# Expansion one-hots made by ScalarE, the aggregate's compares read from PSUM, and the softmax in one PSUM bank, in a five-stage graph kernel

## What is computed

```python
m = xl[src] + xr[dst] + edge_attr @ We.T
score = jnp.where(m > 0, m, 0.2 * m) @ att
smax = jax.ops.segment_max(score, dst, num_segments=N)
es = jnp.exp(score - smax[dst])
denom = jax.ops.segment_sum(es, dst, num_segments=N)
alpha = es / (denom[dst] + 1e-16)
out = jax.ops.segment_sum(alpha[:, None] * xl[src], dst, num_segments=N)
```

## Time and profile before

| | |
|---|---|
| median of 3 runs | 13644.97 us (13634.25 to 13649.05) |
| the profiled execution's own time | 13576.47 us |
| its span, first to last instruction | 13574.4 us |
| PE, PEld | 77%, 64% of the span busy |
| POOL, DVE, ACT | 68%, 63%, 18% |
| mean granted TensorE clock, of full speed | 0.573 |
| HBM traffic | 65 GB/s over the span |

### The profile page before, as it was taken

One profiled execution on the slowest core, in us unless ns is written; L12 is line 12 of the kernel. 1 busy time (PEld: TensorE's weight loads), 2 busy tenths in 40 slices (PEclk: granted clock), 3 DMA queues, 4 the chain that ended last, 5 costly groups with the idle time before them and its releaser, 6 DMA issues. The chain is left out here.

```text
span 13574.4 us, 346433 instructions
## 1 busy us (share of the span) xinstructions
PE 10504.2 (77%) x102671; PEld 8732.6 (64%) x102672; DVE 8519.3 (63%) x15786; ACT 2406.7 (18%) x4954; POOL 9220.1 (68%) x8386
## 2 busy tenths in 40 slices
PE   2388888857888888488888857888888578888872
PEld 1377777746777777377777735777777357777762
DVE  7567777755777777355555544777777446666664
ACT  0011212111111122022222211111111112222220
POOL 0177777756777776577777735777777257777761
PEclk9855556555555555555555555555555555555555
DMA  0333333323333332222222223232222233333320
GB/s 16 84 75 71 73 73 73 73 42 75 72 72 73 73 71 57 39 55 54 55 54 55 54 54 106 77 78 77 77 78 72 69 96 78 78 78 78 78 64 11
DMA packets 771899, 912.63 MB, mean 67 GB/s; under 512 B 400125, under 2 KB 447616, under 8 KB 769760
## 3 DMA queue, kind: packets, MB, share of 16 engines
q0 software_dynamic: 267232, 390.16, 15.0%
q1 hardware_dynamic: 503008, 498.92, 13.0%
HBM read 791.99 MB, written 96.35 MB: 65 GB/s over the span
## 5 line engine op out<-in xcount | busy, mean ns | idle before, releaser
L914 POOL DMA_INDIRECT bs_gat<-table_b,bs_idx x1568 | 1750.7, 1117 | 506.5 <-issue 477.5
L914 POOL DMA_INDIRECT ds_gat<-table_d,ds_idx x1568 | 1749.3, 1116 | 506.7 <-issue 506.7
L914 POOL DMA_INDIRECT as_gat<-table_a,as_idx x1568 | 1740.9, 1110 | 506.6 <-issue 477.5
L914 POOL DMA_INDIRECT es_gat<-table_e,es_idx x1568 | 1725.7, 1101 | 505.6 <-issue 505.6
L914 POOL DMA_INDIRECT cs_gat<-table_c,cs_idx x1568 | 1731.0, 1104 | 491.0 <-issue 491.0
L1174 PE MATMUL ds_psM<-dstW_d,ds_hot 128*128 x9408 | 1252.7, 232 | 194.4 <-DVEq L1107 72.2
L1174 PE MATMUL es_psM<-dstW_e,es_hot 128*128 x9408 | 1253.5, 226 | 175.9 <-issue 65.3
L1174 PE MATMUL cs_psM<-dstW_c,cs_hot 128*128 x9408 | 1232.0, 183 | 182.3 <-DVEq L1100 68.9
L1174 PEld LDWEIGHTS ds_psM<-dstW_d,ds_hot 128*128 128x128 bf16 x9408 | 972.2, 103 | 481.6 <-issue 241.1
L1174 PEld LDWEIGHTS es_psM<-dstW_e,es_hot 128*128 128x128 bf16 x9408 | 962.6, 102 | 480.8 <-issue 224.4
L1174 PEld LDWEIGHTS cs_psM<-dstW_c,cs_hot 128*128 128x128 bf16 x9408 | 967.5, 103 | 473.0 <-issue 223.3
(11 more groups left out here) (758 smaller groups left out, 17937.2 us busy)
## 6 DMA issues: line engine op xcount, KB each, us to landing
as_rank<-rel_d SPq DMA_DIRECT2D x196, 256.0 KB
as_ea<-in_eaT SPq DMA_DIRECT2D x196, 256.0 KB
bs_rank<-rel_d SPq DMA_DIRECT2D x196, 256.0 KB
bs_ea<-in_eaT SPq DMA_DIRECT2D x196, 256.0 KB
cs_rank<-rel_d SPq DMA_DIRECT2D x196, 256.0 KB, 3.2
ds_rank<-rel_d SPq DMA_DIRECT2D x196, 256.0 KB, 3.3
es_rank<-rel_d SPq DMA_DIRECT2D x196, 256.0 KB, 3.4
table_e<-et_st SPq DMA_DIRECT2D x49, 544.0 KB, 2.7
```

The costliest lines, as they stand in the source:

```text
L914: g_.indirect_dma_start(gat[s][:, j, :], None, table, bass.IndirectOffsetOnAxis(ap=idxS[s][:, j:j + 1].bitcast(U32), axis=0)).then_inc(got ...
```

## The change

- `rel` is kept as fp32 instead of bf16, and the interleaved table `rankX` is replaced by `iota`, the numbers 0 to 255, which DVE copies once a stream into a PSUM bank of its own, `psI`.
- `collect_hot` becomes eight compares, one a tile: `psI` (fp32, 256 columns) against one column of `rel`. `ahot` is stored tile by tile, so that the weights of a collect matmul are contiguous; they had a step of 8 elements.
- The expansion's one-hots move from DVE to ACT, as max(0, 1 - (rank - p)²) by two Square and two Relu instructions of 1024 columns, with the partition's number as a pointer bias. They stand at the end of ACT's step.
- The softmax's transposes all go to `psX`, since `psY` gives up its bank to `psI`. The transposing of the next scores waits for `alphad` (alpha copied out) where it waited for `lowered`, and the wait for `alphad` before `give_ends` is left out.

```diff
-            rel=sb("rel", [P, TILES], BF16),
+            rel=sb("rel", [P, TILES]),
-            rankX=sb("rankX", [P, 2 * P, GROUP], BF16),
-            pid=sb("pid", [P, 2]),
+            iota=sb("iota", [P, 2 * P]),
+            pidN=sb("pidN", [P, 2]), one=sb("one", [P, 1]),
...
-        ahot = [sb(f"ahot{s}", [P, 2 * P, GROUP], BF16) for s in range(2)]
+        off = sb("off", [P, 2, GE], BF16)
+        ahot = [sb(f"ahot{s}", [P, GROUP, 2 * P], BF16) for s in range(2)]
...
-        psX, psY = ps("psX"), ps("psY")
+        psX, psI = ps("psX"), ps("psI")
...
             @block.scalar
+                def onehot(it, s):
+                    g = it * RING + s
+                    a.wait_ge(fed[s % 4], it * (3 * FEED) + (s // 4) * FEED + FEED)
+                    wait(a, made, g - 1)
+                    wait(a, hots, g)
+                    for x in range(2):
+                        a.activation(off[:, x, :], rank[s % 4][:, :], ACT.Square, bias=m["pidN"][:, x:x + 1]).then_inc(apart, 1)
+                    for x in range(2):
+                        a.wait_ge(apart, g * 2 + (x + 1))
+                        last = a.activation(hot[s % 2][:, x, :], off[:, x, :], ACT.Relu, bias=m["one"][:, 0:1], scale=-1.0)
+                    last.then_inc(hots, 1)
...
                     if i == 3 and r == 3 and within(xc, CHUNKS):
                         a.wait_ge(backed, xc + 1)
-                        a.activation(alpha[xs][:, 0, :], psY[:, 384:384 + CT], ACT.Copy).then_inc(alphad, 1)
+                        a.activation(alpha[xs][:, 0, :], psX[:, 256:256 + CT], ACT.Copy).then_inc(alphad, 1)
+                    if within(u + 2, GROUPS):
+                        if known(u):
+                            onehot((u + 2) // RING, (u + 2) % RING)
+                        else:
+                            onehot(it if s + 2 < RING else it + 1, (s + 2) % RING)
+                onehot(0, 0)
+                onehot(0, 1)
...
             @block.vector
+                v.tensor_copy(psI[:, 0:2 * P], m["iota"][:, :]).then_inc(xch, 1)
...
-                    for a in range(2):
-                        last = v.tensor_scalar(hot[s % 2][:, a, :], rank[s % 4][:, :], m["pid"][:, a:a + 1], None, ALU.is_equal)
-                    last.then_inc(hots, 1)
...
                 def collect_hot(k, ks):
                     wait(v, summed, k * 2 - 2)
-                    v.tensor_tensor(ahot[ks % 2][:, :, :], over(m["rel"][:, bass.ds(k * GROUP, GROUP)], 1, [P, 2 * P, GROUP]),
-                                    m["rankX"][:, :, :], ALU.is_equal).then_inc(ahots, 1)
+                    for j in range(GROUP):
+                        last = v.tensor_scalar(ahot[ks % 2][:, j, :], psI[:, 0:2 * P], m["rel"][:, bass.ds(k * GROUP + j, 1)], None, ALU.is_equal)
+                    last.then_inc(ahots, 1)
...
             @block.tensor
-                                    last = pe.matmul(sums[h][a][:, bass.ds(w, 1), :], ahot[ks % 2][:, a * P:(a + 1) * P, j],
+                                    last = pe.matmul(sums[h][a][:, bass.ds(w, 1), :], ahot[ks % 2][:, j, a * P:(a + 1) * P],
...
                     if r == 1 and live:
-                        wait(pe, alphad, xc)
                         give_ends(ended, xc + 1, gaveE)
...
                     if r == 0 and live:
                         pe.wait_ge(scored, xc * CG + CG)
-                        wait(pe, lowered, xc)
+                        wait(pe, alphad, xc)
```

More of the change, by code:

```diff
@@ L322, in _ @@
                                 base=0, pattern=[[1, P]], channel_multiplier=-1).then_inc(made, 1)
-                g.iota(m["rankX"][:, :, :], pattern=[[1, 2 * P], [0, GROUP]], base=0, channel_multiplier=0,
+                g.iota(m["iota"][:, :], pattern=[[1, 2 * P]], base=0, channel_multiplier=0,
                        allow_small_or_imprecise_dtypes=True).then_inc(made, 1)
@@ L328, in _ @@
                        allow_small_or_imprecise_dtypes=True).then_inc(made, 1)
-                g.iota(m["pid"][:, :], pattern=[[P, 2]], base=0, channel_multiplier=1,
+                g.memset(m["one"][:, :], 1.0).then_inc(made, 1)
+                g.iota(m["pidN"][:, :], pattern=[[-P, 2]], base=0, channel_multiplier=-1,
                        allow_small_or_imprecise_dtypes=True).then_inc(made, 1)
@@ L848, in stream @@
         masked = [sem(f"masked{s}") for s in range(3)]
-        hots, made, took, scored, sch, xch, ready, blank, wl, pch, sub, past = (
-            sem(n) for n in ("hots", "made", "took", "scored", "sch", "xch", "ready", "blank", "wl", "pch", "sub", "past"))
+        hots, made, took, scored, sch, xch, ready, blank, wl, pch, sub, past, apart = (
+            sem(n) for n in ("hots", "made", "took", "scored", "sch", "xch", "ready", "blank", "wl", "pch", "sub", "past", "apart"))
         turned, ended, gaveE, carried, gaveC, lowered, exped, backed, alphad = (
@@ L931, in step @@
                         a.wait_ge(backed, xc + 1)
-                        a.activation(alpha[xs][:, :, :].rearrange("p h t -> p (h t)"), psY[:, 384:384 + R], ACT.Copy).then_inc(alphad, 1)
+                        a.activation(alpha[xs][:, :, :].rearrange("p h t -> p (h t)"), psX[:, 256:256 + R], ACT.Copy).then_inc(alphad, 1)
                     if within(k, GROUPS):
@@ L1017, in highest_all @@
                     v.wait_ge(gaveC, xc + 1)
-                    v.tensor_copy(carry[:, :], psY[0:R, 258:260]).then_inc(sub, 1)
+                    v.tensor_copy(carry[:, :], psX[0:R, 400:402]).then_inc(sub, 1)
                     v.wait_ge(sub, (xc + 1) * (2 if i == 3 else 1) - (1 if i == 3 else 0))
@@ L1195, in give_ends @@
                     pe.sem_inc(past, 1)
-                    pe.transpose(psY[0:1, 0:R], ends[:, 1:2], m["ident"][0:R, 0:R])
-                    pe.transpose(psY[0:1, P:P + R], ends[:, 0:1], m["ident"][0:R, 0:R]).then_inc(sem_out, 1)
+                    pe.transpose(psX[0:1, P:P + R], ends[:, 1:2], m["ident"][0:R, 0:R])
+                    pe.transpose(psX[0:1, 2 * P:2 * P + R], ends[:, 0:1], m["ident"][0:R, 0:R]).then_inc(sem_out, 1)
                 def give_carry(sem_in, value, sem_out):
@@ L1202, in give_carry @@
                     for x in range(2):
-                        last = pe.transpose(psY[0:R, 258 + x:259 + x], car[0:1, x, 0:R], m["ident"][0:1, 0:1])
+                        last = pe.transpose(psX[0:R, 400 + x:401 + x], car[0:1, x, 0:R], m["ident"][0:1, 0:1])
                     last.then_inc(sem_out, 1)
@@ L1232, in step @@
                         pe.wait_ge(normed, xc + 1)
-                        pe.matmul(psY[:, 384:384 + CT], Al[:, :], m["quart"][:, :], start=True, stop=True).then_inc(backed, 1)
+                        pe.matmul(psX[:, 256:256 + CT], Al[:, :], m["quart"][:, :], start=True, stop=True).then_inc(backed, 1)
                     if within(k - 1, GROUPS):
```

19 lines of the change are left out of this document (4 added, 15 removed).

## The result

| | before | after |
|---|---|---|
| median of 4 runs each | 13647.0 us | 13908.3 us (13902 to 13913) |
| ratio | | 1.019 (95%: 1.0175 to 1.0211) |
| the profiled execution's own time | 13576.5 us | 13913.4 us |
| PE, PEld busy | 77%, 64% | 74%, 61% |
| DVE, ACT, POOL busy | 63%, 18%, 68% | 69%, 46%, 59% |

The forecast was 13855, slower with 0.7. It came out slower, 53 us above the forecast and inside the range. The two profiled executions differ by more, 337 us, a ratio of 1.025.

The account below looks back on a forecast made before the run. POOL's gather issue was taken as the bound, PE 4% behind. Chunks of 45.5 us, 48.6 in d, sum to 230.6 against 226.3: +210 us, 13787, raised 0.5% to 13855; range 13430 to 14340.

Parts of the forecast that it names:

- POOL sets 45.3 us a chunk: Before the change, POOL's issue of gathers, which waits for nobody, takes 45.3 us a chunk in stage a.
- PE is only 4% behind: PE's chunk in a takes 43.26 us where it hardly waits, against 45.3 on average; freeing POOL wins at most that.
- Compares 0.40 each, 3.2 us a group: DVE's eight new PSUM compares take 0.40 us each, 3.2 a group, adding 1.3 us a group to DVE.
- ACT 1.15 us an instruction, 4.3 a group: ACT's four one-hot instructions of 1024 columns take 1.15 us each, 4.3 a group back to back, bounds 4.0 and 4.7.
- The ring over two steps: Dependency loop from one-hots through expand, collect, compares and split to one-hots: 21.25 us, 10.6 a step, against PE's 10.62.
- The Exp step: Once a chunk, all stages: Exp precedes ACT's one-hots, so the next expand stalls 1.9 us more, taken as 2.2.
- d's second stall: Stage d's step with the reciprocal: alpha precedes the one-hots, delaying the next expand 3.8 us, taken as 3.1 a chunk.
- Collect 2.95: PE's 48 collect matmuls, with contiguous weights, take 2.95 us instead of 3.14, a gain all eaten in the two-step ring.
- the sum of a, b, c and e: Chunk in these stages: 43.3 + 2.2 = 45.5 us; each stage longer by less than 30 us.
- Rival A: Faster: POOL was the bound and is freed, chunks fall to 42.5 us, 12970 us; chance with its half 0.20.
- Rival B: Much slower: the new compares hold POOL up, 12.5 us a group, chunks of 50, 14800 us; chance 0.08.
- C: No change: gains of collect and POOL cancel d's stalls, within 27 us of 13645; chance 0.10.

Follow-up runs that it names:

- e4: The kernel before with only the hardware loop's body doubled: 13571.0 us, 0.9994 of the kernel before.
- e10: The kernel before, with expand's matmuls reading the window at constant column 0 (scores differ): 13559.1 us, 0.9997 of the kernel before.
- e3: The changed kernel with the one-hots made three groups ahead instead of two, in three buffers: 13365.4 us, 0.9852 of the kernel before.
- e7: The changed kernel with one Square and one Relu a group instead of two each (scores differ): 13450.7 us, 0.9916 of the kernel before.
- e11: The changed kernel with the one-hots issued before Exp and d's alpha in ACT's step: 13891.3 us, 1.0239 of the kernel before.
- e1: The changed kernel with the one-hots back on DVE, at the head of its step: 13548.0 us, 0.9989 of the kernel before.
- e2: The kernel before with only the one-hots moved to ACT: 13798.8 us, 1.0171 of the kernel before.
- e8: e3 with the hardware loop's body doubled, 7 turns of 24 steps: 13174.5 us, 0.9701 of the kernel before.
- e12: e3 with the hardware loop's body four times as long, 3 turns of 48 steps: 13047.2 us, 0.9617 of the kernel before.
- e9: e3 with expand's matmuls reading the window at constant column 0 (scores differ): 12872.0 us, 0.9479 of the kernel before.
- e5: The changed kernel with the eight compares reading the column numbers from SBUF instead of PSUM: 13803.9 us, 1.0175 of the kernel before.

## Why the prediction was right, and where not

- *What bounds the kernel before.* "POOL sets 45.3 us a chunk" holds: e4 and e10. "PE is only 4% behind" rested on one quiet chunk of 43.26. PE's own mean includes 15 turns of 4 to 5 us in 49 chunks, 1.2 to 1.5 us each: 44.5 to 44.8, 1 to 2% behind, not 4.
- *Compares 0.40 each, 3.2 us a group.* Measured 0.392, 3.14. *ACT 1.15 us an instruction, 4.3 a group:* 1.13, and 4.25 from the first's start to the last's end (1499.13 to 1503.38). Both prices, from the nearest rows, were right within 3%. That DVE's extra 1.3 us a group would stay below PE's step holds inside the streams, but not at their ends: 52 us together, which the sum did not have. The Trainium skill's rule that Relu and add belong on VectorE, up to about three times faster in bf16 (ScalarE: Activation LUTs, Rules for kernel authors), agrees on ratio: a pass over 1024 columns is 1.04 us on ACT and 0.40 on DVE. ACT needed four passes for DVE's two; the prediction's "harsher" set four passes beside two.
- *The ring over two steps, 21.25 us, just ties with PE.* The one-hots come 0.56 us before the expand in steps without Exp: no loss, little slack.
- *The Exp step, 1.9, taken 2.2.* Measured 2.0 to 2.3 a chunk in a; e3 removes it by place, e7 by length. e11 could not, as shown. Quiet chunks in a: 44.8 to 45.4 where 45.5 was forecast.
- *d's second stall, 3.1.* Measured 3.24 there, and 2.66 to 3.12 after Exp, where 2.2 was taken. Two waits of that size were forecast as 5.3 and cost 5.9 to 6.4 before what PE makes up; d's mean chunk is 48.7, forecast 48.6.
- *Collect 2.95.* Measured 2.82 in a and b, 2.90 in c and e, 2.74 in d. "All eaten" was right, but the eater is PE's sequencer; e1 and e3, which have no stall, show no gain from it either.
- *The step that failed* is the sum of a, b, c and e: 43.3 + 2.2 = 45.5, the other stages longer "by less than 30" us. The chunks are 46.0, 46.0, 45.7 and 46.0, and from first gather to last flush the stages are 34 to 60 us longer; d's 169 are half of the whole, not "nearly all". Missing was the turn of the loop. As long as POOL sets the mean a turn is caught up; with PE as the bound it is added, 1.2 us a chunk. A quiet chunk of PE's was put beside POOL's mean, which is two different kinds of number. The smaller quiet chunk took 0.4 of it back, and shorter chunks at the ends of the streams some more; the rest stayed out: 6.0 us a chunk over the five stages against 4.3 forecast, 83 us.
- *Luck in the number.* The sum was +210 us on the profiled execution, and the profiled executions differ by 337, so it had 62% of the loss. The 53 us between 13855 and 13908 are fewer than the 126 between 13787 and 13913 because 0.5% (68 us) was added for the median of before. The changed kernel had no such surplus: its median is 13908 and its profiled execution 13913.
- *Rival A* (12970) could not have come even without the stall: its 42.5 us had neither the turn nor the sequencer in it. e3, the change with the stall taken away, gives 13365, 1.5% under the kernel before. *Rival B* is excluded: the mean gather fell from 1110 to 989 ns. *C* is what e1 came to. Of the signs of being wrong none came: the gathers' spans of a to c are 2201, 2203 and 2185 us, their mean fell, PE waits for ACT, and the collect is shorter.
- Why the ratio is 1.019 in the one measurement and 1.025 in the other stays open. The changed kernel takes nearly the same in both (13908 and 13919); it is the kernel before that took 13634 to 13650 in four runs and 13553 to 13601 in all others, the profiled execution among them.

## What to carry to other kernels

When work moves to an idle engine, what counts is the dependency behind which it is placed: 4.3 us a group on an engine that was 18% busy cost 1.7% by themselves (e2), and one step and one buffer more turned the loss of the whole change into a gain of 1.5%. Before saying how far the second engine is behind the first, take its mean over whole turns of the loop, not a quiet stretch, and look whether its matmuls or its addresses set its pace. When one bound is lifted, a cost that was caught up in its shadow (the loop's turn) appears in full.

## What the hardware showed that was not expected

- At each turn of the hardware loop PE stands 4.9 us before an expand that otherwise follows at once (1480.58 and 1618.08 above); in e8 and e12 the device time falls by 5.1 and 5.7 us for each turn taken away, 4.6 to 4.7 of them PE's idle time at the turn.
- A matmul of 64 columns whose moving operand's address comes from a register takes 136 ns, with a constant address 57 ns (e9), with the same weight loads.
- The step between a tile's weights, 8 elements or none, is worth 0.3 us in 48 matmuls of 65 columns: 3.13 us in before and e2, 2.82 in the change, e1 and e3.
- A compare of 256 fp32 columns takes 0.392 us from PSUM and 0.263 from SBUF; from SBUF the longest gather beside it takes 3.49 us and not 1.68 (e5).
